# Four fused attention layers on one core: layer 1's twelve PSUM uses dealt to three banks, its border with layer 0 and its first step reordered

## The reference, cut to what matters

```python
# layer 0: non-local attention, then batch norm over ALL batches
w_y  = einsum('oc,btc->bot', Wz, softmax(phi @ theta) @ g_x) + bz
mean, var = mean(w_y, axis=(0, 2)), var(w_y, axis=(0, 2))
latents = gamma * (w_y - mean) * rsqrt(var + 1e-5) + beta + x
# layer 1: attention of the latents over [context, latents], 16 heads of 32, then an MLP
h = concatenate([ctx, latents], axis=1)           # 256 rows a batch here
q, k, v = latents @ q_w + q_b, *(h @ kv_w + kv_b)
attn = softmax(where(mask, q @ k.T / 32, -inf)) @ v
a = rmsnorm(attn @ out_w + out_b + latents, postnorm_w)
out = gelu(a @ mlp_w1 + mlp_b1) @ mlp_w2 + mlp_b2 + latents    # 512 -> 2048 -> 512
```

## Time and profile before

| what | value |
|---|---|
| median of 3 runs | 2327.11 us (2327.05 to 2329.89) |
| the profiled execution's own time | 2325.5 us |
| its span in the trace | 2323.7 us |
| TensorE busy over the span | 2164.6 us (93%) |
| VectorE, ScalarE, GpSimd busy | 49%, 50%, 24% |
| layer 0 | 0 to about 196 us |
| layer 1 | about 196 to 1132 us |
| layers 2 and 3 | about 1132 us to the end |

### The profile page before, as it was taken

The page is one execution under the profiler, slowest core; times in us unless marked ns, Lnnn a source line. Parts: engine busy times, 40 slices in busy tenths (PEclk is TensorE's granted clock), DMA queues, the critical chain, the costliest instruction groups (busy, mean ns, idle before and its releaser), DMA issues.

```text
span 2323.7 us, 56522 instructions
## 1 busy us (share of the span) xinstructions
PE 2164.6 (93%) x22208; PEld 1578.5 (68%) x22208; DVE 1132.4 (49%) x3132; ACT 1164.6 (50%) x3500; POOL 567.2 (24%) x573
## 2 busy tenths in 40 slices
PE   7886799999999999998579999999999999999986
PEld 3444576666667766665367787777777877778754
DVE  4664333333333333333334566555666665566643
ACT  4553344444444444443123665655566565566554
POOL 0001000000001000000143444433344444344420
PEclk9998899999999999999779999999999999999998
DMA  5531333333333333334501001011110101110000
GB/s 167 169 112 62 103 100 102 94 95 105 101 99 103 95 91 91 91 83 119 163 16 22 18 21 27 16 26 22 27 22 21 27 16 27 22 22 20 21 19 10
DMA packets 188378, 149.06 MB, mean 64 GB/s; under 512 B 85280, under 2 KB 163488, under 8 KB 185888
## 3 DMA queue, kind: packets, MB, share of 16 engines
q1 hardware_dynamic: 177920, 115.49, 19.5%
q10 hardware_dynamic: 8032, 18.35, 2.2%
q0 software_dynamic: 2240, 12.58, 1.6%
HBM read 96.04 MB, written 46.14 MB: 61 GB/s over the span
## 4 chain that ended last, share of the span: by engine, by line
PE 47%; ACT 1%; DVE 1%; issue 1%; POOL 0%; POOLq 0%; DVEq 0%; ACTq 0%
PE bank L1561 13%; PE bank L1567 12%; PE bank L1554 4%; PE quad L1689 4%; PE quad L1694 2%; PE quad L1808 1%; PE bank L1824 1%; PE quad L1685 1%; PE bank L1590 1%; PE quad L1610 1%; PE bank L1712 1%; PE quad L1699 1%; PE bank L1724 1%; PE bank L1629 1%; PE bank L1637 1%
## 5 line engine op out<-in xcount | busy, mean ns | idle before, releaser
L782 PE MATMUL bank<-normedT,mlp_w 128*128 128x128 f32 x2048 | 242.5, 278 | 18.7 <-ACT geluT L878 17.9
L782 PEld LDWEIGHTS bank<-normedT,mlp_w 128*128 128x128 f32 x2048 | 233.7, 193 | 31.7 <-ACT geluT L878 20.7
L792 PE MATMUL bank<-mlp_w,geluT 128*128 128x512 f32 x512 | 224.7, 592 | 0.0
L2005 ACT ACTIVATE scores<-scores,nmax 128x128 f32<-128x128 f32 x512 | 198.3, 396 | 2.5 <-DVE nmax L2267 2.5
L1493 POOL TENSOR_TENSOR k_even_odd<-k_even_odd,decay_products 128x512 f32<-128x512 f32 x80 | 98.1, 1226 | 327.3 <-PE quad L1689 251.8
L792 PEld LDWEIGHTS bank<-mlp_w,geluT 128*128 128x128 f32 x512 | 95.0, 190 | 108.1 <-issue 108.1
L958 DVE CUSTOM_DVE_ANT_0 probs<-quad,neg_mask 128x256 f32<-128x256 f32 x256 | 90.8, 420 | 110.1 <-PE quad L737 110.1
L886 ACT ACTIVATE probs<-probs,nmax 128x256 f32<-128x256 f32 x256 | 126.6, 496 | 12.2 <-DVE nmax L958 11.7
L1421 POOL TENSOR_TENSOR gn_rstd<-gn_var_eps,halfs 128x32 f32<-128x32 f32 x16 | 87.0, 5435 | 170.3 <-DVE gn_var_eps L2190 170.3
L2267 DVE CUSTOM_DVE_ANT_0 scores<-quad,mask 128x128 f32<-128x128 f32 x512 | 110.9, 286 | 31.7 <-PE quad L1808 31.7
L2155 DVE TENSOR_TENSOR rT<-rT,decay_products 128x256 f32<-128x256 f32 x96 | 40.9, 426 | 175.0 <-PE quad L1689 72.0
(11 more groups left out here) (241 smaller groups left out, 4502.4 us busy)
## 6 DMA issues: line engine op xcount, KB each, us to landing
l_blocks<-probs_turned_blocks SPq DMA_DIRECT2D x128, 256.0 KB, 2.7
probsT<-l_blocks SPq DMA_DIRECT2D x256, 128.0 KB, 3.6
x_in<-in_x SPq DMA_DIRECT2D x32, 256.0 KB, 2.9
mlp_w<-in_mlp_w POOLq DMA_DIRECT2D x8, 1024.0 KB, 5.6
ctx_in<-in_ctx SPq DMA_DIRECT2D x16, 256.0 KB, 2.9
l_out<-wy ACTq DMA_DIRECT2D x16, 256.0 KB, 2.2
wy_in<-l_out SPq DMA_DIRECT2D x16, 256.0 KB, 3.8
hT<-in_ctxT SPq DMA_DIRECT2D x16, 256.0 KB, 3.5
```

The source lines that it names most:

```text
L782: mm = nc.tensor.matmul(ps[:, f * P:(f + 1) * P], mlp_w1[:, c, m * P:(m + 1) * P], nT[:, c, :], start=(c == 0), stop=(c == NC - 1))
L792: mm = nc.tensor.matmul(PS[M.bank][:, :], gT[:, f, :], mlp_w2[:, f, :], start=(f == 0), stop=(f == NF - 1))
L2005: ac = nc.scalar.activation(s, s, ACT.Exp, bias=nmax[:, k, 2 * c + e:2 * c + e + 1], scale=-1.0, accum_out=rsum[:, kv, gr:gr + 1])
```

## The change

Three parts. **Banks:** the ten uses of banks 5 and 6 and the two of bank 7 become twelve uses dealt to three banks, each bank with its own pair of semaphores and a fixed order: bank 5 holds q, v0, h0, h3; bank 6 holds k0, the turned normalised rows (tn), h1, the MLP output (out); bank 7 holds k1, v1, h2, the next latents. A use begins when the use before it in its own bank has been copied out. **Border:** batch norm's last operations move from the end of layer 0's block to the beginning of layer 1's; batch 0's loads for layer 1 move from the beginning of layer 1's block to the end of SyncE's stream in layer 0; values 0 of batch 0 become TensorE's first work in layer 1 (its copy on ScalarE stands between the batch norm and the copy of the latents). **First step:** step 1 is taken out of TensorE's loop, and both halves of batch 1's keys stand in front of attention 0.

```diff
-    def __init__(self, ready, free, banks, first, per_loop):
-        self.ready, self.free, self.banks, self.first, self.per_loop = ready, free, banks, first, per_loop
...
-        at = n if i is None else self.first + n
-        before = n if i is None else self.first + (i - 1) * self.per_loop + n
-        return Slot(self.banks[at % len(self.banks)], before + 1, before + 1 + len(self.banks))
+    def __init__(self, ready, free, bank, front, loop):
+        self.ready, self.free, self.bank, self.front, self.loop = ready, free, bank, front, loop
+
+    def at_front(self, name):
+        return Slot(self, self.front.index(name))
+
+    def at_loop(self, i, name, missing=0):
+
+        return Slot(self, len(self.front) + (i - 1) * len(self.loop) + self.loop.index(name) - missing)
...
+    def __init__(self, lane, before):
+        self.ready, self.free, self.bank = lane.ready, lane.free, lane.bank
+        self.claim, self.made, self.read = before + 1, before + 1, before + 2
...
@@ -179,6 +179,9 @@
 
                     sp.wait_ge(G.ready, G.written(i - 1, 1))
                     load(i)
+                load_ctx1(sp, 0)
+                sp.wait_ge(s_store, 32)
+                load_x1(sp, 0)
...
-                pool.wait_ge(s_bnv, 2)
-                nc.gpsimd.tensor_tensor(bnt[:, 1:2], bnt[:, 0:1], halfs[:, 0:1], ALU.pow).then_inc(s_bnv, 1)
...
-
                 dve.wait_ge(s_stat, B)
-                nc.vector.bn_aggr(mv[:, :], stats[:, :, :].rearrange("p b s -> p (b s)")).then_inc(s_bnv, 1)
-                dve.wait_ge(s_bnv, 1)
...
-        A = Lane(*S["a"], [5, 6], len(FRONT), len(LOOP))
+        rings = dict(s=([0, 1, 2, 3], NG), o=([4], 2))
+        S = {k: (sem(f"l1_{k}_psum_ready"), sem(f"l1_{k}_psum_free")) for k in rings}
+        FRONT = {5: ["v0", "q", "v1"], 6: ["k0", "next_latents"], 7: ["latents", "k1"]}
+        LOOP = {5: ["q", "v0", "h0", "h3"], 6: ["k0", "tn", "h1", "out"], 7: ["k1", "v1", "h2", "next_latents"]}
+        BEHIND = {5: 2, 6: 1, 7: 3}
+        A = {k: Lane(sem(f"l1_bank{k}_ready"), sem(f"l1_bank{k}_free"), k, FRONT[k], LOOP[k]) for k in LOOP}
 
         def slot(i, name):
...
             if isinstance(i, int) and i == 0:
-                return A.use(None, FRONT.index(name))
-            if isinstance(i, int) and i == B:
-                return A.use(B, LOOP.index(name) - LOOP.index("h0") - 1)
-            return A.use(i, LOOP.index(name))
+                return next(u for u in A.values() if name in u.front).at_front(name)
+            u = next(u for u in A.values() if name in u.loop)
+            return u.at_loop(i, name, BEHIND[u.bank] if isinstance(i, int) and i == B else 0)
...
                 O = ring("o")
-                load_x(0)
-                load_ctx(0)
-
...
                 def loads(i):
                     sp.wait_ge(s_lat, i)
-                    load_x(i)
+                    load_x(sp, i)
 
                     sp.wait_ge(s_negm, i)
-                    sp.wait_ge(A.free, slot(i - 1, "v1").read)
-                    load_ctx(i)
+                    sp.wait_ge(slot(i - 1, "v1").free, slot(i - 1, "v1").read)
+                    load_ctx(sp, i)
...
                 def next_latents_b2(i):
                     pool.wait_ge(s_latb2n, i + 1)
                     if not isinstance(i, int) or i > 0:
-                        pool.wait_ge(M.free, M.read(i - 1, 2))
+                        u = slot(i, "out")
+                        pool.wait_ge(u.free, u.read)
...
+                pool.wait_ge(s_bnv, 2)
+                nc.gpsimd.tensor_tensor(bnt[:, 1:2], bnt[:, 0:1], halfs[:, 0:1], ALU.pow).then_inc(s_bnv, 1)
                 latents(0)
...
-                pe.sem_inc(A.free, len(A.banks))
-                SR, O, M = (ring(k) for k in "som")
+                for u in A.values():
+                    pe.sem_inc(u.free, 1)
+                SR, O = (ring(k) for k in "so")
...
+                def copied(u):
+                    pe.wait_ge(u.free, u.read)
+
                 def turn_latents(i):
-                    ps = claim(latents_slot(i))
+                    u = latents_slot(i)
+                    ps = claim(u)
...
                 def values(i, n):
-                    ps = claim(slot(i, f"v{n}"))
+                    if isinstance(i, int) and i == 0 and n == 0:
+                        pe.wait_ge(s_ctx, 16)
+                    u = slot(i, f"v{n}")
+                    ps = claim(u)
...
                 def hidden(i, j):
                     if j == 0:
-                        pe.wait_ge(M.free, M.read(i, 1))
-                    ps = claim(slot(i + 1, f"h{j}"))
+                        copied(slot(i + 1, "tn"))
+                    u = slot(i + 1, f"h{j}")
+                    ps = claim(u)
...
                 def mlp_out(i, j):
+                    u = slot(i + 1, "out")
                     if j == 0:
-                        b = M.next()
-                        pe.wait_ge(M.free, M.count)
-                    pe.wait_ge(A.free, slot(i + 1, f"h{j}").read)
+                        claim(u)
+                    copied(slot(i + 1, f"h{j}"))
                     for f in range(4 * j, 4 * j + 4):
-                        mm = nc.tensor.matmul(PS[M.bank][:, :], gT[:, f, :], mlp_w2[:, f, :], start=(f == 0), stop=(f == NF - 1))
+                        mm = nc.tensor.matmul(PS[u.bank][:, :], gT[:, f, :], mlp_w2[:, f, :], start=(f == 0), stop=(f == NF - 1))
                     if j == 3:
-                        mm.then_inc(M.ready, 1)
...
+                def batch(i, first=False, last=False):
                     queries(i)
+                    if first:
+                        keys(i, 0)
+                        keys(i, 1)
                     attend(i - 1)
-                    keys(i, 0)
+                    if not first:
+                        keys(i, 0)
                     project(i - 1)
-                    keys(i, 1)
+                    if not first:
+                        keys(i, 1)
                     values(i, 0)
...
+                values(0, 0)
                 turn_latents(0)
                 queries(0)
                 keys(0, 0)
                 keys(0, 1)
                 scores(0, 0)
-                values(0, 0)
                 scores(0, 1)
                 values(0, 1)
                 turn_latents(1)
-                with pe.Fori(1, B - 1) as i:
+                batch(1, first=True)
+                with pe.Fori(2, B - 1) as i:
                     batch(i)
                 batch(B - 1, last=True)
...
                 def batch_norm(i, first=False):
                     act.wait_ge(s_in, 32 * i + 32)
-                    if not first:
-
+                    if first:
+                        act.wait_ge(s_bnv, 6)
+                    else:
...
                 def store(i):
-                    act.wait_ge(M.free, M.read(i, 2))
+                    u = slot(i + 1, "out")
+                    act.wait_ge(u.free, u.read)
                     act.dma_start(l1_out[i], xo[:, :]).then_inc(s_store, 16)
...
                 batch_norm(0, True)
+                copy_v(0, 0)
                 copy_latents(0)
                 copy_q(0)
                 copy_k(0, 0)
@@ -924,8 +926,7 @@
                 batch_norm(1)
                 for g in range(4):
                     exps(0, g)
-                for n in range(NK):
-                    copy_v(0, n)
+                copy_v(0, 1)
                 for g in range(4, NG):
                     exps(0, g)
...
+                def batch_norm_factors():
+                    nc.vector.bn_aggr(mv[:, :], stats[:, :, :].rearrange("p b s -> p (b s)")).then_inc(s_bnv, 1)
...
                 dve.sem_inc(s_store, 16)
+                batch_norm_factors()
                 mask(0)
...
+        hT = sb1("hT", [P, NC, 2 * P])
+        s_in1 = sem("l1_inputs_loaded")
+        s_ctx = sem("l1_context_loaded")
+        s_mask = sem("l1_mask_loaded")
+
+        def load_x1(sp, i):
+            sp.dma_start(wyin[:, :], l0_out[i]).then_inc(s_in1, 16)
+            sp.dma_start(xin1[:, :], a["x"][i]).then_inc(s_in1, 16)
+
+        def load_ctx1(sp, i):
+            sp.dma_start(maski[:, :], a["mask1"][i].unsqueeze(0).to_broadcast([P, P])).then_inc(s_mask, 16)
+            sp.dma_start(hT[:, :, 0:P], a["ctxT"][i]).then_inc(s_ctx, 16)
```

146 lines of the change are left out of this document (70 added, 76 removed).

## The result

The kernel after takes 2298.72 us (median of 4 runs, 2296.95 to 2301.31) against 2327.08 before (4 runs, 2324.7 to 2329.89): a ratio of 0.9879, 95% interval 0.9861 to 0.9896, or 28.4 us less. The profiled execution took 2297.31 us over a span of 2295.5. The forecast was 2298.9. Measured once more beside other kernels, it took 2301.47 us (4 runs, 2300.45 to 2302.6) against 2325.57 (7 runs, 2321.16 to 2328.71): 0.9894, interval 0.9877 to 0.991, or 24.1 less. So the gain is known to a few us only, and that 28.4 lies within 0.2 of the forecast 28.2 is luck. It is luck in the sum too, as the stages will show: the loop's term was too small, the terms of border and first step were too large, a cost in the first batch was missing, and stages that the change does not touch made up the rest.

What follows compares the result with a forecast made beforehand. TensorE, busy 93% of the span, was taken to set the pace, with hidden 3 waiting for gelu in layer 1's steps. Loop 18.9 + border 3.7 + first batch 0.5 + first step 5.1 = 28.2 us, giving 2298.9; range 2293 to 2307.

Steps and rivals of the forecast that it cites:

- The loop: MLP in layer 1's steps: hidden 3 no longer waits for the second gelu; 14 x 1.35 = 18.9 us, bounds 15.5 and 20.4.
- All four margins: Next waits in the loop stay covered: MLP out 2.5, keys 0 4.6, attention's second half 0.8 to 2.7, others several microseconds.
- the smallest margin, 0.8 to 2.7: Attention's second half in the loop: the moves of probabilities land 0.8 to 2.7 us before it needs them.
- Step 15: Layer 1's end: step 15's saving is lost, because attention 15's second half, which waited 1.80 us for the moves, waits longer.
- The border: Layer 0 to 1: earlier start, values 0 taking the cold clock, queries 0 at full speed; 3.7 us, bounds 2.4 and 5.2.
- The first batch: Scores half 1 no longer behind values 0: 0.5 us (0.3 to 0.6); a slower values 1 covered by VectorE's idle time.
- The first step: Batch 1's keys in front of attention 0, hidden in idle time: 5.1 us, the middle of 5.95 to 4.25.
- The cold time: First step's projection: half-speed clock costs 0.8 us if back at 257.7, up to 2.5 if the new gap delays it.
- its two cases: Border: the clock's release point varies, so it could give either bound, and the sum 26.9 or 29.7 instead of 28.2.
- no wait for the moves in the loop (2317.8): Rival, attention in the loop: late moves of probabilities use up the margin; 9.3 us left, 2317.8; chance 0.07.
- no late eviction: Rival, bank 6: VectorE's MLP output eviction over 4.6 us late makes keys 0 wait; 2340.9 at 3.0 us; chance 0.03.
- The cold clock at the front: Rival, border and first step: new idle pieces keep the clock at 0.50, together 2 us; 2306.2; chance 0.10.

Runs made afterwards that it cites:

- idle turns: values 1 between plus unused turnings of the constant identity on TensorE ahead of attention's second half and behind the last projection: 2295.28 us, 0.9863 of before.
- hidden 3 behind hidden 1, clean: Changed kernel with hidden 3 again behind hidden 1 and the MLP output behind hidden 0; queries and keys 0 change banks: 2319.65 us, 0.997 of before.
- no keys in front: Changed kernel with step 1's keys behind attention 0 and the projection again: 2304.72 us, 0.9911 of before.
- the first swap: Changed kernel with hidden 3 in bank 6, the MLP output in bank 7, the next latents in bank 5: 2353.61 us, 1.0122 of before.
- chain in layer 0: Changed kernel with values 0 behind scores half 0 and batch norm's last operations back in layer 0; loads stay moved: 2298.66 us, 0.9884 of before.
- context late: Changed kernel with batch 1's mask and context loaded behind the first half's moves of batch 0: 2300.01 us, 0.9883 of before.
- values 1 between: Changed kernel with values 1 of batch 0 between the two halves of its scores: 2298.49 us, 0.9885 of before.
- mended: together with 60 instead of 54 idle turns before attention 0's second half, and the 22 for batch 15 alone: 2293.43 us, 0.9862 of before.
- together: chain in layer 0 plus idle turns of the identity at border, first latents, attention 0 and 15, and the last projection: 2295.96 us, 0.987 of before.

## Why the prediction was right, and where not

- **The loop: mechanism right, size 8% off.** 14 x 1.35 = 18.9 was forecast, 20.4 measured, 1.46 a step. The term took the start of hidden 3 alone, 1.36 earlier. By 10.82 / 96 a matmul takes 0.1127 us in the string, so its start comes 8.60 - 7.21 = 1.39 earlier, and hidden 3 itself takes 3.61 to the next group instead of 3.67. The prediction's 1.36 for a step was therefore no bound. Its range of 15.5 to 20.4 reached the measured 20.4 only because it counted fifteen steps.
- **What is late next: right.** All four margins held; the list of waits in the loop is empty. That attention in the loop does not wait for the moves shows that the smallest margin, 0.8 to 2.7, was real.
- **Step 15: right that most of its saving is lost, wrong that nothing more is.** The wait grew from 1.80 to 2.85, which takes 1.05 of the 1.46 (2.6 to 3.7 in the other executions with the new loop). I left out the clock. The projection behind the wait took 5.12 to 6.59 us in all eight executions with the new loop and no idle turns, and where the end column reads over 92, that cost 2 to 3 us. It is tempting to blame the longer wait, and waits of 3.2 us and more all had 6.4 or more behind them. But hidden 3 behind hidden 1, clean, waited 1.7 and had 5.06, before waited 1.80 and had 3.67, no keys in front had 6.53 behind 2.69, and the first swap, whose attention did not wait there at all, had 3.67. So it is shown that the half-speed clock costs this, since the idle turns take it away, and not that the change brought it. That it shows little in after's end column (90.08) is because layer 2's first turning came 1.3 us sooner behind the MLP than in before's profile (44.06 against 45.35), which no run explains (44.0 to 45.0 in all the other executions without idle turns).
- **The border: 3.7 forecast, 3.5 measured,** by the steps foreseen: 194.14 for layer 1's first issue (195.8 less the 1.54 by which this execution is ahead is 194.3), values 0 in 5.58 (3.67 + 2.4 = 6.1 forecast) but 0.95 behind that issue, where I had let it start at once, queries in 3.81. What the sum hid is that it has three parts of different sign: +3.3, -1.1 and +1.3. The prediction took the chain's move for a gain, because layer 1 then begins 0.9 earlier, and gave the loads no term of their own; chain in layer 0 shows that the loads alone bring 3.3 and that the chain's move costs 1.1.
- **The first batch: the step that failed.** The prediction put the cost of the new idle time at nothing, as covered. It forecast 0.5 gained; measured 0.4 gained and 1.6 lost. I checked the cover on VectorE's timeline alone, and there it holds: the second half is normalised at 232.4 and turned at 238.05. The prediction asked what a lower clock would do to values 1 (1.4 us, 5.10 against 3.70), and not to scores half 1, which stands ahead of them, now runs at half speed and heads the chain (0.9). Nor did I look at SyncE, where the context load waits for the copy of values 1 and so comes right ahead of the block stores (0.9 until the second half is turned).
- **The first step: 5.1 forecast, 4.1 measured** (4.5 in four other executions with the same front). Keys, eviction and the RMS chain (0.53 against 0.5) are as costed. The cold time was taken at the middle, 1.65; it was 6.06 - 3.60 = 2.5, its upper bound: 8.3 - 1.05 - 0.5 - 2.5 = 4.25.

So the terms miss by +1.5, -0.2, -1.7 and -1.0, which with +0.3 for the end of layer 1 is -1.1, and the 1.1 of the stages outside the change made it even. That is chance, since those stages move by more than this between executions. The Trainium skill ("TensorE: Matmul & The Clock Gate", Part 1) says that the point at which sustained work releases the clock varies from run to run; values 0, the same matmuls in the same place, took 5.58 and 5.30 us in the two executions of after and 5.11 to 5.45 in six others, which agrees. Its rule that idleness throttles agrees with the end of layer 1: 1.00 until the waits of 2.85 and 0.95 us, then 0.63 and 0.52. By its two cases my sum would have been 26.9 or 29.7; with gains of 28.4 and 24.1 in two measurements, neither can be told from 28.2.

Of the rivals three fell: no wait for the moves in the loop (2317.8), no late eviction, and hidden 3's bank was what ended the wait. The cold clock at the front fell in its size, since border and first step give 7.6 and not 2, but a new idle piece did hold the clock at 0.50 in scores half 1, and that is part of what was lost.

## What to carry to other kernels

When a buffer must be waited for, look which of its previous users is late and deal the buffers by that, one lane each; an alternation gives every use the predecessor that happens to stand two before it, and a blind swap can make another use wait for the late one. Cost a reordering also by what the clock does in the idle time that it makes or lengthens, at the end of the loop as well as in front: some tens of turnings of a constant in an otherwise idle stretch were worth 3 us at each of two places in one kernel, and next to nothing at one of them in another, where they ended 1.4 us too soon. And check a cover on every queue of the chain, the one that issues the transfers above all, since a load that waits for a copy stands ahead of all that is issued behind it.

## What the runs showed of the hardware that was not expected

- The same eight matmuls lose between 1.5 and 2.9 us in the last projection (5.12 to 6.59 us against 3.67), from one kernel's execution to the next, behind waits of 2.6 to 3.7 us; behind 1.7 us they lost 1.4, and behind 1.8 us, or no wait, nothing. What decides was not found out.
- One context load issued 0.60 us ahead of the four block stores, instead of 1.84, cost 1.2 us in their landing (3.87 against 2.64 until the moves are issued). Issued behind the moves (context late) or 5.3 us ahead of the stores (values 1 between), it cost them nothing (2.66 and 2.65).
- Eight moves take 3.72 to 4.07 us to issue in the first batch, but 4.80, 4.93 and 5.07 in the three cases in which a packet of the instruction queue falls into the issue (context late, mended, together). In the latter two a second such packet comes just behind the issue of the second half's moves, at 245.5 and 246.0, and the longest of their landings is 5.6 and 5.7 us; in chain in layer 0, which differs from them by idle turns alone, it is 4.1. Their chain to attention 0 is 1.9 and 2.2 us longer, 0.4 and 0.6 of it before the second half is turned and 1.5 and 1.6 behind. That the packets are the cause was not tested.
